# Latent queries of passes two to four by seven block products per pair of heads

## What is computed

```python
xn = layernorm(x)
q = (xn @ wq)                                   # 16 heads of 128 + 64 (rope) columns
kva = xn @ wkv_a; ckv = rmsnorm(kva[:, :128]) * kv_norm_scale; k_pe = rope(kva[:, 128:])
k_nope, v = split(ckv @ wkv_b)                  # per head 128 + 128
scores = (q_nope . k_nope + rope(q_pe) . k_pe) * 192 ** -0.5, causal
attn = softmax(scores) @ v; attn_out = attn @ wo
ffn = xn @ sum(factors) / sqrt(8) + bias
out = x + attn_out + ffn
```

## Time and profile before

| what | value |
|---|---|
| median of 3 runs | 1498.38 us (1497.08 to 1500.48) |
| span of the profiled execution, first to last instruction | 1496.9 us |
| TensorE / DVE / ACT / GpSimd busy | 98 / 68 / 65 / 61 % |
| granted clock of TensorE, mean | 1.000 |
| pass one, two, three, four from the starts of their units | about 55 to 597, to 1005, to 1301, to 1488 us |

### The profile page before, as it was taken

One profiled execution on the slowest core, in us unless ns is written; L12 is line 12 of the kernel. 1 busy time (PEld: TensorE's weight loads), 2 busy tenths in 40 slices (PEclk: granted clock), 3 DMA queues, 4 the chain that ended last, 5 costly groups with the idle time before them and its releaser, 6 DMA issues.

```text
span 1496.9 us, 25751 instructions
## 1 busy us (share of the span) xinstructions
PE 1469.3 (98%) x7908; PEld 755.5 (50%) x7908; DVE 1014.5 (68%) x2563; ACT 965.7 (65%) x2404; POOL 911.3 (61%) x919
## 2 busy tenths in 40 slices
PE   6999999999999999999999999999999999999998
PEld 5544555555555545445444444445545555555554
DVE  7877677877777766656556565556666666676777
ACT  7877767677876567566566666665546665654554
POOL 3688777776665456575465656566645655664553
PEclk9999999999999999999999999999999999999999
DMA  6599999988777597787577677886856677754564
GB/s 202 152 199 203 211 193 186 191 163 158 157 157 132 127 193 149 140 178 139 118 145 141 137 133 145 173 151 130 162 112 136 137 139 152 156 141 95 115 132 110
DMA packets 646615, 227.84 MB, mean 152 GB/s; under 512 B 599376, under 2 KB 612176, under 8 KB 646096
## 3 DMA queue, kind: packets, MB, share of 16 engines
q1 hardware_dynamic: 646480, 226.20, 74.2%
HBM read 65.67 MB, written 17.83 MB: 56 GB/s over the span
## 4 chain that ended last, share of the span: by engine, by line
PE 92%; POOL 2%; DVE 2%; ACT 2%; DMA 1%; issue 1%; SPq 0%; POOLq 0%; DVEq 0%; ACTq 0%
PE ps L426 18%; PE ps L428 18%; PE ps L427 18%; PE ps L577 7%; PE ps L582 7%; PE ps L583 7%; PE ps L578 7%; PE ps L579 7%; POOL st L1408 2%; ACT ex L812 1%; DMA acc<-x_in 0%; DVE stats L944 0%; PE ps L450 0%; DVE acc L1227 0%; DMA pT<-st 0%
## 5 line engine op out<-in xcount | busy, mean ns | idle before, releaser
L1408 POOL TENSOR_TENSOR st<-ex,st 128x512 f16<-128x512 f32 (+3 forms) x640 | 637.8, 1015 | 488.9 <-ACT st L822 478.8
L812 ACT ACTIVATE ex<-ps,nm,scales 128x512 f32<-128x512 f32 (+3 forms) x640 | 452.0, 709 | 456.3 <-DVE nm L1193 439.8
L1174 DVE TENSOR_REDUCE gm<-ps 128x1 f32<-128x512 f32 (+1 forms) x384 | 249.0, 669 | 170.0 <-PE ps L583 166.0
L822 ACT ACTIVATE st<-ex 128x512 f16<-128x512 f32 (+3 forms) x640 | 343.0, 562 | 6.1 <-ACT ex L812 0.4
L577 PE MATMUL ps<-kTh,q 128*128 128x512 f16 (+3 forms) x640 | 222.3, 347 | 4.5 <-ACT ex L812 2.1
L426 PE MATMUL ps<-pT,vH 128*128 128x512 f16 (+3 forms) x640 | 222.1, 347 | 2.9 <-DMA pT<-st 2.9
L582 PE MATMUL ps<-kRh,q 128*128 128x512 f16 (+3 forms) x640 | 222.2, 347 | 0.0
L583 PE MATMUL ps<-kRl,q 128*128 128x512 f16 (+3 forms) x640 | 222.1, 347 | 0.0
L579 PE MATMUL ps<-kTh,q 128*128 128x512 f16 (+3 forms) x640 | 222.1, 347 | 0.0
L578 PE MATMUL ps<-kTl,q 128*128 128x512 f16 (+3 forms) x640 | 222.1, 347 | 0.0
L427 PE MATMUL ps<-pT,vH 128*128 128x512 f16 (+3 forms) x640 | 222.1, 347 | 0.0
(11 more groups left out here) (202 smaller groups left out, 2144.3 us busy)
## 6 DMA issues: line engine op xcount, KB each, us to landing
wA<-w_abs SPq DMA_DIRECT2D x48, 256.0 KB, 2.9
wV<-w_vo SPq DMA_DIRECT2D x48, 256.0 KB, 2.9
pT<-st SPq DMA_TRANSPOSE x640, 3.2
fland<-factors_in SPq DMA_DIRECT2D x28, 256.0 KB, 3.1
wP<-w_pe SPq DMA_DIRECT2D x24, 256.0 KB, 3.0
wsq<-wq_in SPq DMA_DIRECT2D x16, 256.0 KB, 3.8
wso<-wo_in SPq DMA_DIRECT2D x16, 256.0 KB, 3.0
w_abs<-wA SPq DMA_DIRECT2D x16, 256.0 KB, 2.2
```

Of the source, the lines that this page charges most:

```text
L812: e.activation(ex[:, n % NEX, 0:keys], s_bank(n)[:, 0:keys], ACT.Exp, bias=nm[:, (i * QT + r) % 4:(i * QT + r) % 4 + 1], scale=scales[:, p ...
L822: e.activation(stage(n, keys)[:, :, 0, :], ex[:, n % NEX, 0:keys].rearrange("p (t n) -> p t n", n=P), ACT.Copy).then_inc(z["a_pH"], 1)
L1174: e.tensor_reduce(m, b, AX_X, ALU.max).then_inc(z["v_max"], 1)
L1408: e.tensor_tensor(s[:, :, 1, :], ex[:, n % NEX, 0:keys].rearrange("p (t n) -> p t n", n=P), s[:, :, 0, :], ALU.subtract).then_inc(z["g_pL" ...
```

## The change

Heads 2g and 2g+1 of passes two to four share one calculation. Their weights are a matrix of 2 x 2 blocks (two heads x two halves of the width, 256 wide) and the tokens one of 2 x 2 blocks (two halves of the width x two halves of 256 tokens). Strassen's scheme makes the four blocks of the result from seven block products (m1 to m7). A block product is 2 k-blocks x 3 = 6 matmuls of 256 columns, so a pair of heads has 42 matmuls of 256 columns in place of 24 of 512. m1, m6, m5, m3 are accumulated in one bank, m7 and m4 in another, m2 has a third. Between them ACT copies the running sum out ("snapshot", f32 in SBUF) before the next product is added, DVE adds m2, m7 or m4 to a snapshot, ACT writes the high part and GpSimd the low part of the block of `q` (c11, c22, c21); c12 is read from the bank by ACT (high) and DVE (low).

The work is spread over the odd unit 2g-1 and the even unit 2g:

| | row 0 | row 1 | row 2 | row 3 |
|---|---|---|---|---|
| odd unit, TensorE | scores, m1, out, m2 | scores, m6, out | scores, m5, out | scores, out, pv, m3 |
| odd unit, others | snapshot m1; DVE adds m2 | c11 high, snapshot m6; c11 low | snapshot m5 | c12 high (ACT), c12 low (DVE) |
| even unit, TensorE | scores, m7, out | scores, m4, out | scores, out | scores, out, (pe), pv |
| even unit, others | DVE adds m7 | c22 high and low; DVE adds m4 | c21 high and low | |

The first products (for heads 16 and 17) lie in units 15 and 16. In pass one each pair of heads gets four sums of weight blocks: ACT copies both `wabs` banks as f32 (16 copies of 512 columns), DVE and GpSimd make two subtractions of 256 columns each per pair, ACT four high parts and GpSimd four low parts of 256 columns. They are stored (512 KB a pair) beside the blocks, of which the one that no product needs is left out. Later passes load 896 KB a pair where two loads of 256 KB stood. The sums of tokens for a pass are made in the pass before it: GpSimd 14 operations of 512 columns and ACT 4, over nine steps. The tokens are double-buffered. The factor XS is 2^9 in place of 2^10, and many semaphores that DVE waits on for itself become one (`v_own`).

```diff
+STEPS = {"p_m": ("m1", "m2", "m6", "m5", "m3", "m7", "m4"), "a_m": ("m1", "c11", "m6", "m5", "c12", "c22", "c21"),
+         "v_m": ("c11", "c12", "c22", "c21"), "g_m": ("c11", "c22", "c21")}
 def fills(i, r):
+    if r == 1:
+        if H <= i + 1 < NU and i % 2:
+            out += [("c11", (i + 1) // 2), ("m6", (i + 1) // 2)]
+        if H <= i < NU and i % 2 == 0:
+            out += [("c22", i // 2), ("m4", i // 2)]
+    if r == 2:
+        if H <= i + 1 < NU and i % 2:
+            out.append(("m5", (i + 1) // 2))
+        if H <= i < NU and i % 2 == 0:
+            out.append(("c21", i // 2))
     if r == 0:
-        if 1 <= i < NU - 1:
+        if 1 <= i < H - 1:
             out.append(("q", i + 1))
+        if H <= i + 1 < NU and i % 2:
+            out.append(("m1", (i + 1) // 2))
+        if H <= i < NU and i % 2 == 0:
+            out.append(("m7", i // 2))
...
+    if r == 0 and H <= i + 1 < NU and i % 2:
+        out.append(("m2", (i + 1) // 2))
...
+    if r == 3 and H <= i + 1 < NU and i % 2:
+        out.append(("m3", (i + 1) // 2))
+    for m in range(G0):
+        if r == 3 and i == sum_slot(m):
+            out.append(("sum", m))
+        if r == 0 and i == sum_slot(m) + 1:
+            out.append(("sum_hi", m))
+        if r == 1 and i == sum_slot(m) + 1:
+            out.append(("sum_lo", m))
...
+            # TensorE
+            def blocks(kind, o, w, b, first):
+                for n in range(2):
+                    ins = three(o[:, 0:HC], [weight_block(w, a)[:, n * P:(n + 1) * P] for a in range(2)],
+                                [b[a][:, n, :] for a in range(2)], first and n == 0, n == 1, kind not in ("m1", "m2", "m7"))
+                ins.then_inc(z["p_m"], 1)
...
+                elif kind == "m5":
+                    e.wait_ge(z["a_m"], done("a_m", "m6", g))
+                    blocks("m5", bank(("m1", g)), S1, [summed(k, 1, a) for a in range(2)], False)
+                elif kind == "m3":
+                    e.wait_ge(z["a_m"], done("a_m", "m5", g))
+                    blocks("m3", bank(("m1", g)), S4, [token_block(k, a, 1, 1) for a in range(2)], False)
...
+            # ACT
+            def snapshot(kind, g):
+                n = g - G0 + 1
+                e.wait_ge(z["p_m"], done("p_m", kind, g))
+                ...
+                e.activation(snap[kind], bank(("m1", g))[:, 0:HC], ACT.Copy, scale=BACK).then_inc(z["a_m"], 1)
+            def block_high(kind, g):
+                if kind == "c12":
+                    e.wait_ge(z["p_m"], done("p_m", "m3", g))
+                    e.activation(q_half(i, 0, 1), bank(("m1", g))[:, 0:HC], ACT.Copy, scale=BACK).then_inc(z["a_m"], 1)
...
-                    early = ("q", "wo", "sqv") + (("sq1",) if i == 0 else ())
+                    early = ("q", "wo", "sqv", "m1", "c11", "m6", "c22") + (("sq1",) if i == 0 else ())
...
+            # DVE, a fill of row 3 of the odd unit
+            def block_low(g):
+                e.wait_ge(z["a_m"], done("a_m", "c12", g))
+                e.scalar_tensor_tensor(out=q_half(2 * g, 1, 1), in0=bank(("m1", g))[:, 0:HC], scalar=BACK,
+                                       in1=q_half(2 * g, 0, 1), op0=ALU.mult, op1=ALU.subtract).then_inc(z["v_m"], 1)
...
+            # GpSimd
+            def sums_low(m):
+                ...
+                for n, (at, f) in enumerate(((S3, f1[:, 0:HC]), (S1, f1[:, HC:CH]), (S2, f0[:, 0:HC]), (S4, f0[:, HC:CH]))):
+                    e.wait_ge(z["a_sum"], 4 * m + n + 1)
+                    e.tensor_tensor(weight_block(at, 1), f, weight_block(at, 0), ALU.subtract).then_inc(z["g_sum"], 1)
```

More of the change, by code:

```diff
@@ L1 @@
+import itertools
 from contextlib import ExitStack
@@ L232, in bank_order, with take @@
             pre.append(("q", 0))
-    body = [k for i in range(NU + 2) for r in range(QT) for k in fills(i, r) if k[0] in IN_BANKS or k == ("nrm", 2)]
-    return pre, body
+    bank, before, last, held = {}, {}, {}, {}
+    def take(key, b):
+        bank[key], before[key], last[b] = b, last.get(b), key
+    for n, key in enumerate(pre):
+        take(key, [MB, MB + 1, MB + 2, OB][n % 4])
+    free = [MB + n for n in range(MBANKS)]
+    for i in range(NU + 2):
+        for r in range(QT):
+            for key in fills(i, r):
+                if key[0] in IN_BANKS or key == ("nrm", 2):
+                    b = free.pop(0)
+                    take(key, b)
+                    if key[0] in LEFT:
+                        held[LEFT[key[0]], key[1]] = b
+                    else:
+                        free.append(b)
+                elif key in held:
+                    free.append(held.pop(key))
+    return pre, bank, before
 def build(nc, x, wq, wkv_a, wkv_b, wo, kvs, factors, bias, rope_t, rope_n, out):
@@ L424, in _, with three @@
         def _(e):
[L425 to L428, removed]
+            def three(o, a, b, first=True, last=True, more=False):
+                e.matmul(o, a[0], b[0], start=first, stop=False, skip_group_check=more)
+                e.matmul(o, a[0], b[1], start=False, stop=False, skip_group_check=more)
+                return e.matmul(o, a[1], b[0], start=False, stop=last, skip_group_check=more)
             def count(key):
@@ L433, in free_bank @@
             def free_bank(key):
[L435 to L438, removed]
+                user = used_before[key]
+                if user and user[0] in LAST_READ:
+                    e.wait_ge(z["v_m"], done("v_m", LAST_READ[user[0]], user[1]))
+                elif user:
+                    e.wait_ge(z["v_" + user[0]], count(user))
+                    if user[0] == "wabs":
+                        e.wait_ge(z["a_wf"], count(user))
                 return bank(key)
             def outputs_bank_left():
-                last = [k for k, b in zip(pre_uses, bank_of) if b == OB][-1]
+                last = [k for k in pre_uses if bank_of[k] == OB][-1]
                 e.wait_ge(z["v_" + last[0]], count(last))
@@ L574, in scores @@
                     e.wait_ge(z["v_kT"], (p + 2) * QT // 2)
-                if r == 0 and p == 0:
+                if r == 0 and p == 0 and i < H:
                     e.wait_ge(z["v_q"], i + 1)
+                if r % 2 == 0 and p == 0 and i >= H:
+                    engine, part = (("g_m", "c22" if r else "c21") if i % 2 else ("v_m", "c12") if r else ("g_m", "c11"))
+                    e.wait_ge(z[engine], done(engine, part, i // 2))
                 e.matmul(b, q[:, i % 2, 0, qs], kTh[:, ks], start=True, stop=False)
@@ new lines, in sums_high @@
+            def sums_high(m, which):
+                if which < 2:
+                    e.wait_ge(z["v_sum"], 2 * m + 2)
+                else:
+                    e.wait_ge(z["g_sum"], 6 * m + 2)
+                if m and which == 0:
+                    e.wait_ge(z["d_sS"], 16 * m)
+                f = weights_f(m, 1 if which < 2 else 0)
+                if which < 2:
+                    parts = ((S3, slice(0, HC)), (S1, slice(HC, CH)))
+                else:
+                    parts = ((S2, slice(0, HC)), (S4, slice(HC, CH)))
+                at, cols = parts[which % 2]
+                e.activation(weight_block(at, 0), f[:, cols], ACT.Copy).then_inc(z["a_sum"], 1)
@@ L833, in fill @@
                     q_latent(n)
+                elif kind == "wabs":
+                    weights_sums(n)
+                elif kind == "sum_hi":
+                    for which in range(4):
+                        sums_high(n, which)
+                elif kind == "tok":
+                    k, s = n
+                    for t, at in TOKENS_HIGH:
+                        if at == s:
+                            tokens_high(k, t)
+                elif kind == "m1":
+                    snapshot("m1", n)
+                elif kind == "m6":
+                    snapshot("m6", n)
+                elif kind == "m5":
+                    snapshot("m5", n)
+                elif kind == "m3":
+                    block_high("c12", n)
+                elif kind in ("c11", "c22", "c21"):
+                    block_high(kind, n)
                 elif kind == "parts":
@@ L937, in _, with own @@
         def _(e):
+            chained = itertools.count(1)
+            def own():
+                return next(chained)
             def norm_stats(p2):
@@ L1387, in rope_parts @@
                     e.wait_ge(z["g_pL"], piece(i - 1, r, chunk(i - 1)) + 1)
+                    if r == 1 and i >= H:
+                        e.wait_ge(z["g_m"], done("g_m", "c22" if i % 2 else "c11", i // 2))
                 hi = q[:, i % 2, 2, :]
```

363 lines of the change are left out of this document (293 added, 70 removed).

## The result

The changed kernel takes 1645.88 us (median of 4 runs, 1644.35 to 1646.2) against 1498.99 us for the kernel before (1497.08 to 1500.48, 4 runs on the same chip): 1.0983 times as long, 95 % interval 1.0967 to 1.0998. Forecast were 1606 us and 1560 to 1645. The span of the profiled execution is 1643.7 us, 146.7 us more than before.

The account below looks back on a forecast made before the run. TensorE, busy 98 % of the span, was taken to bound the kernel. Terms -13.4 + 31.7 + 72.0 + 13.6 + 3.7 = +107.6 us on 1496.9 gave 1604.5, plus 1.5 for the median 1606; range 1560 to 1645.

Parts of the forecast that it names:

- products on TensorE: Passes two to four: seven block products replace two latent queries, saving 0.56 us a pair, 13.4 us over 24 pairs.
- odd starts: Row 0 of odd units: the removed query covered the first head output's wait for DVE's `oT`; 31.7 us of waits.
- even starts: Even units' first output waits because DVE's c12 low part, waiting for ACT, precedes maxima, bias and `oT`; 72.0 us.
- m5 behind its copy: m5 waits for ACT's copy of the sum before it, in passes three and four; 13.6 us together.
- units 0 and 1: Start of pass one: added GpSimd subtractions lengthen the chain by 3.7 us, bounds 0 and 5.
- the clock: TensorE may lose rate after idle stretches; called possible, but the sum had nothing for it.
- rival (d): Matmuls after each long wait run at half rate: 27 us in pass two (1633), 82 in all (1688); chance 0.07.
- Rows 14: Prologue matmuls after 2.2 us idle, at 1.2 columns a nanosecond, read as showing a loss of rate after waits is possible.
- Later in pass one POOL and ACT have gaps: Gaps of 2 to 4 us in every later unit of pass one, so the other sums cost nothing.
- (b): Rival: the wait on c12 is hidden, even units start like odd ones, 31 in place of 72.0: 1565 us; chance 0.10.
- (c): Rival: the first head output finds `oT` ready without its cover, and m5 its copy: 1489 us; chance 0.05.
- (e): Rival: more waits than found, such as 0.8 us more in each unit, 38 us: 1644 us; chance 0.11.

Follow-up runs that it names:

- products last: Changed kernel with DVE's c12 low part later, no head output in row 0, m6 and m4 behind outputs, m5 behind outputs and values: 1516.0 us.
- pass one alone: Kernel before, with the weight sums of pass one made and stored but never read: 1503.17 us.
- Both forms: Old: two tensor inputs in DVE's last denominator step. New: one tensor and a per-partition scalar; put into the changed kernel, 1642.04 us.
- the first edit: Changed kernel with DVE's low part of c12 moved to the even unit's row 0, behind the low part of `oT`: 1563.94 us.
- the best one: The products last run with the second unit of each pass (17, 33, 49) arranged as the other odd ones: 1513.28 us.

## Why the prediction was wrong

The direction was right, the mechanism of the waits too, and their sum almost exact. In us:

| term | forecast | measured | from |
|---|---|---|---|
| products on TensorE | -13.4 | -13.4 | unit 38 without waits (products last): 17.74 against 19.02, 2 x 0.66 - 2.59 |
| odd starts | 31.7 | 29.8 | 10.4, 10.2, 8.0 and 1.2 in unit 15 |
| even starts | 72.0 | 69.8 | 27.2, 21.2, 21.4 |
| m5 behind its copy | 13.6 | 14.2 | 8.9 and 5.3 |
| units 0 and 1 | 3.7 | 3.7 | unit times |
| units 3 and 7 | 0 | 5.0 | unit times |
| the clock | 0 | 37.2 | half rate, 24 stretches |
| sum | 107.6 | 146.3 | span: 146.7 |

**The step that failed** is the clock's: the sum took matmuls behind a long wait to go at full rate. The prediction had seen slow matmuls in the prologue and wrote that "this sum has nothing for it", and gave the case that has it 0.07. In the changed kernel 23 of the 24 even starts were followed by slow matmuls, and one wait for m5. That makes 37.3 us, less than half of the 82 that rival (d) took for all starts: the stretch at half rate covers some 3.3 us (792.22 to 795.57), of which half is lost, and (d) had taken 3.4 us of loss, a figure for which it names no row. The Trainium skill ("TensorE: Matmul & The Clock Gate", HAM oscillation) says that idle stretches between bursts bring the clock down and each burst then starts slow. The changed kernel agrees, in 23 of its 24 even starts. The waits put into the kernel before agree in 12 of 24 only.

Rows 14 were also read for more than they show. They stand behind an idle stretch, but TensorE was slow before it. Its first matmuls in the trace of the kernel before, from 6.92 us on (128 columns in f32), are 0.213 us apart, and the same ones 0.109 apart from 20.43 on, so it had not yet left the lower rate. And the trace holds no record of the granted clock before 19.21 us, so the 1.00 that the view prints there isn't a measurement.

**A second, smaller step** is "Later in pass one POOL and ACT have gaps [...] so the other sums [...] cost nothing". In the trace of pass one alone the later sums did cost nothing. But they and the later start of units 0 and 1 took GpSimd's gap ahead of unit 3. In the kernel before it stood idle for 1.74 us until 147.54; in the changed one it works on without a gap until 158.12, and a small DVE instruction that met it without harm (0.19 us, begun 0.98 us into one of its operations) now begins 0.38 us into one and stalls. That is 5.0 us in this trace. The Trainium skill ("SBUF — State Buffer", Who interferes with whom) says that DVE and GpSimd share one pair of ports and one blocks the other for a whole instruction, when DVE has two SBUF inputs or is in a mode with two ports, which `tensor_scalar` can enter too. Both forms stalled here, which fits, but that the ports are the cause is argued and not shown. The page has the block last for one instruction; here it lasts over the rest of one GpSimd instruction and the four behind it (5.47 us), and the measurement decides. What makes the difference between 0.77 and 5.47 us I can't say.

The waits came out in their places. The forecast counts from the start at which an output was due, so it is compared from start to start; the view's idle times are some 0.16 us less. At odd starts 1.28, 1.28 and 1.18 us were measured in units 23, 39 and 55, against 1.27, 1.51 and 1.16. m5 waits 0.96 and 0.72 against 1.0 and 0.8. Even starts wait 3.29, 2.49 and 2.69 against 3.6, 2.7 and 2.85. There DVE's c12 ended where the forecast had it (in unit 22 at 789.56 - 785.83 = 3.73 us into the row, against 3.75); too long were the maxima and the bias behind it, counted as 2.2 us and measured as 1.9. One start was far off the other way: unit 16 has 4.1 us where the forecast had 1.2, because the longer row 3 ahead of it covered nothing (ACT reads `oT` 2.4 us into the row, as in unit 22) and ACT then makes squares of weights (L968) before c12's high part, which starts 3.76 us into the row and not 2.88. So that the even starts' sum is only 2.2 us off is in part luck.

The other rivals: (b), c12 hidden, isn't this kernel, but it is what the first edit makes of it, 1563.9 against its 1565. (c) is out, since `oT` was ready at no start. (e) gave the right time, 1644, for a wrong reason: no further waits of 0.8 us in each unit were there.

What stays open is when exactly a wait of 2 to 4 us is followed by half rate, and what sets a stall of DVE beside GpSimd; also whether a version faster than before exists: it would have to bring what the best one still adds, 21.0 us of waits, 1.9 of half rate and pass one's, under the 13.4 us that the products save.

## What to carry to other kernels

Work that is taken off the busiest engine may have been the cover of a wait. Before it goes, take what the next instruction waits for, and on which in-order engine something new is put ahead of it: here one DVE instruction ahead of the maxima cost six times what the change saves. And a wait of 2 us or more on TensorE may not be paid with its own length alone: up to 1.7 us came on top for the matmuls at half rate behind it, while waits of up to 1.8 us brought none in the first edit's trace. Shorten such a wait, or fill it, even with useless matmuls.

## What was unexpected of the hardware

- Adding 63 us of matmuls made the kernel 38 us faster, by half rate that did not come.
- The half rate can begin at once after a wait (792.22) or a microsecond later (780.42), and of equal waits of 2.91 us only some bring it.
- DVE's 0.16 us instruction took 5.47 us beside back-to-back operations of GpSimd, and 0.77 us in another kernel, begun at the same point of the same operations.
